# A two-layer decoder on one core: block ends without GpSimd's drain, transposed probabilities in the score banks, and a root computed two steps earlier

## What is computed

```python
x = x + linear_attention(layernorm(x))                    # layer 0
x = x + cross_attention_16_heads(layernorm(x), ctx)       # layer 0, head size 16
h = layernorm(x)                                          # layer 0, 16 experts
val, idx = top_k(sigmoid(h @ gate_w + gate_b), 2)
x = x + h + mlp_shared(h) + sum(val / sum(val) * expert[idx](h))
x = x + self_attention_16_heads(layernorm(x))             # layer 1, head size 64
# layer 1, cross attention with 8 heads of size 64, its own norms
q = (layernorm(layernorm(x)) * g1 + b1) @ Wq
k, v = split((layernorm(ctx) * g2 + b2) @ Wkv)
x = x + softmax(q k^T / 8) v @ Wout + bout
# layer 1, 8 experts with a capacity of int(1.2 * 2 * 112 / 8) = 33 rows each
x = x + experts_1(layernorm(x))
```

## Time and profile before

| | us |
|---|---|
| median of 3 runs | 1809.79 (1804.32 to 1810.95) |
| profiled execution | 1809.45 |
| its span | 1807.8 |

### The profile page before, as it was taken

One profiled execution on the slowest core, in us unless ns is written; L12 is line 12 of the kernel. 1 busy time (PEld: TensorE's weight loads), 2 busy tenths in 40 slices (PEclk: granted clock), 3 DMA queues, 4 the chain that ended last, 5 costly groups with the idle time before them and its releaser, 6 DMA issues. The chain is left out here.

```text
span 1807.8 us, 36461 instructions
## 1 busy us (share of the span) xinstructions
PE 1646.2 (91%) x12689; PEld 1358.2 (75%) x12689; DVE 1113.7 (62%) x2668; ACT 884.1 (49%) x2541; POOL 554.3 (31%) x846
## 2 busy tenths in 40 slices
PE   5997599999998888799999969999999889999998
PEld 3665467777776577588888757777777679999987
DVE  4776467777777544367777656666666544444464
ACT  2333356555555233155555544444444456666644
POOL 2122222443343334422221111233223256444410
PEclk8999689999999789999999979999999989999999
DMA  8000323444450353200000020000000031123001
GB/s 255 0 0 1 113 83 120 131 129 129 129 171 12 121 168 124 63 11 17 12 12 1 1 85 20 18 14 14 18 18 1 1 140 71 71 76 134 1 1 42
DMA packets 87549, 114.29 MB, mean 63 GB/s; under 512 B 4804, under 2 KB 76696, under 8 KB 87160
## 3 DMA queue, kind: packets, MB, share of 16 engines
q1 hardware_dynamic: 82280, 99.56, 17.0%
q0 software_dynamic: 5136, 12.98, 2.2%
HBM read 64.68 MB, written 47.84 MB: 62 GB/s over the span
## 5 line engine op out<-in xcount | busy, mean ns | idle before, releaser
L1051 ACT ACTIVATE wide<-ps,c_negmax 112x375 f32<-112x375 f32 x256 | 143.7, 581 | 2.1 <-DVE c_negmax L1157 2.1
L1262 PEld LDWEIGHTS ps<-const,wide 112*125 112x125 f32 x768 | 97.8, 193 | 47.2 <-DVE c_pT L1179 27.5
L1157 DVE TENSOR_REDUCE c_negmax<-ps 112x2 f32<-112x750 f32 x128 | 114.2, 934 | 25.4 <-PE ps L1293 25.4
L1262 PE MATMUL ps<-const,wide 112*125 112x112 f32 x768 | 116.1, 289 | 3.4 <-ACT wide L1051 2.0
L2101 PE MATMUL ps<-xnT,wide 128*128 128x224 f32 x512 | 108.6, 361 | 4.7 <-ACT e_gate_up L1877 4.3
L1893 ACT ACTIVATE s_probs<-ps,s_negmax 112x112 f32<-112x112 f32 x256 | 86.7, 364 | 37.2 <-DVE s_negmax L1959 37.2
L2101 PEld LDWEIGHTS ps<-xnT,wide 128*128 128x128 f32 x512 | 93.5, 190 | 9.8 <-ACT e_gate_up L1877 5.5
L1352 PE MATMUL ps<-parts 128*125 128x256 f32 (+1 forms) x480 | 91.0, 327 | 5.5 <-DVE X L1108 2.4
L3041 DVE TENSOR_TENSOR e_hid_low<-xnT,e_hid_high 128x528 fp32r<-128x528 f32 x56 | 41.2, 735 | 82.7 <-ACT e_hid_high L2941 82.7
L1039 ACT COPY c_pT<-ps 125x672 f32<-125x672 f32 x64 | 46.1, 720 | 82.0 <-PE ps L1262 82.0
L1352 PEld LDWEIGHTS ps<-parts 128*125 128x125 f32 (+1 forms) x480 | 71.8, 196 | 13.1 <-DVE wide L1103 4.7
(11 more groups left out here) (493 smaller groups left out, 5074.0 us busy)
## 6 DMA issues: line engine op xcount, KB each, us to landing
expert_rows<-d_zero SPq DMA_DIRECT2D x16, 2240.0 KB, 11.5
c_ctx_in<-in_ctx SPq DMA_DIRECT2D x32, 375.0 KB
e_x_in<-expert_rows SPq DMA_DIRECT2D x43, 128.0 KB, 2.1
expert_rows<-e_y POOLq DMA_DIRECT2D x43, 128.0 KB, 2.1
e_w_gate_even<-in_L_ffn_w_gate SPq DMA_DIRECT2D x4, 1024.0 KB, 5.1
e_w_fc_even<-in_L_ffn_w_c_fc SPq DMA_DIRECT2D x4, 1024.0 KB, 7.2
e_w_proj_even<-in_L_ffn_w_c_proj SPq DMA_DIRECT2D x4, 1024.0 KB, 9.6
c_kv<-in_L_ffn_w_gate SPq DMA_DIRECT2D x4, 1024.0 KB, 5.0
```

Of the source, the lines that this page charges most:

```text
L1051: last = nc.scalar.activation(probs[:, g % 2, r, :], ps[:T, r, 0:S], ACT.Exp, bias=negmax[:, par, h:h + 1], accum_out=sums[:, par, h:h + 1])
L1157: nc.vector.tensor_reduce(negmax[:, par, h:h + 3:2], ps[:T, 2 * piece:2 * piece + 2, 0:S], AX.X, ALU.max, negate=True).then_inc(max_done, 1)
L1262: last = nc.tensor.transpose(ps[:KC, bank + r % 2, k * T:(k + 1) * T], probs[:, g % 2, r, k * KC:(k + 1) * KC], ident[:T, :T])
```

## The change

In context attention 1 the transposed probabilities of head x go into score bank x instead of bank 4, and TensorE no longer waits for the copy before. In experts 0 the root moves from behind the store of block 33 to behind that of block 31, and `ContextEntry.STEPS` goes from 10 to 13, which moves the normalized rows from the steps 35 to 37 to the steps 38 to 40.

```diff
-        block = ctx.enter_context(nc.Block())
+        block = ctx.enter_context(nc.Block(no_gpsimd_drain=True))
...
-        with nc.Block() as block:
+        with nc.Block(no_gpsimd_drain=True) as block:
...
-                if j == CONTEXT_AT + 5:
+                if j == CONTEXT_AT + 3:
                     entry.power(pool, 0)
...
-    STEPS = 10
+    STEPS = 13
...
-    BANK_PT, BANK_O, BANK_SIDE = 4, 5, 6
+    BANK_O, BANK_SIDE = 5, 6
...
                     act.wait_ge(pT_mm, 4 * (2 * i + g) + x + 1)
-                    nc.scalar.copy(pT[:, x, :], ps[:KC, BANK_PT, 0:SC]).then_inc(pT_ready, 1)
+                    nc.scalar.copy(pT[:, x, :], ps[:KC, x, 0:SC]).then_inc(pT_ready, 1)
...
                     dve.wait_ge(pT_mm, 4 * (2 * i + g) + x + 1)
-                    nc.vector.tensor_copy(pT[:, x, :], ps[:KC, BANK_PT, 0:SC]).then_inc(pT_ready, 1)
+                    nc.vector.tensor_copy(pT[:, x, :], ps[:KC, x, 0:SC]).then_inc(pT_ready, 1)
...
                 pe.wait_ge(exp_done, n + 1)
-                if not (first(i, g) and x == 0):
-                    pe.wait_ge(pT_ready, n)
                 for k in range(NK):
-                    last = nc.tensor.transpose(ps[:KC, BANK_PT, k * T:(k + 1) * T], probs[:, x, k * KC:(k + 1) * KC], ident[:T, :T])
+                    last = nc.tensor.transpose(ps[:KC, x, k * T:(k + 1) * T], probs[:, x, k * KC:(k + 1) * KC], ident[:T, :T])
                 last.then_inc(pT_mm, 1)
```

## The result

| | before | after |
|---|---|---|
| median of 3 runs, us | 1809.79 | 1785.39 |
| lowest and highest | 1804.32 to 1810.95 | 1784.55 to 1786.39 |
| profiled execution, its span | 1809.45, 1807.8 | 1784.55, 1782.9 |

The account below looks back on a forecast made before the run. It took TensorE's pace to bound the two layer-one attention stages. 1809.45 - 10.9 (banks) - 1.85 (root) + 2.8 (block ends) = 1799.5 us, set to 1799.8 for the median; range 1788.5 to 1804.0.

Parts of the forecast that it names:

- Part 3, the block ends: At block ends without Pool's drain, L118's drain does the same work behind the first barrier: cost 2.8 us.
- nobody pays: At three block ends, the removed drain's time vanishes and L118's stays at 40 ns: -6.25 us, 1790.8 in all; chance 0.25.
- the 2 us of clock: In context attention 1's tail, fewer gaps may keep TensorE's higher clock: up to 2 us gained, taken as 0.
- Part 1, steady iterations: Context attention 1, iterations 1 to 13: no wait for the probabilities' copy, 0.44 us gained each, 5.7 us together.
- Its last iteration: Context attention 1, iteration 15: copies no longer waited for, values start 1.95 us earlier; 4.0 us gained over both halves.
- Part 2, the root: Experts 0: power runs earlier and rows later, so the 3.48 us step loses its wait; 1.85 us gained.
- The slower rival: After self-attention 1's longer pause, context attention stays at the lower clock; an iteration costs 17 us, 1816.8; chance 0.04.
- The beat stays: Context attention 1's steady iterations gain nothing, other waits replacing the stall; only the last two gain, 5.2 us: 1805.5; chance 0.11.

Follow-up runs that it names:

- the added meeting: The changed kernel with one more plain all-engine barrier in front of the clearing of the semaphores; 1800.59 us against 1785.39 of the changed kernel.

## Why the prediction was wrong

It forecast 1799.8 and a range of 1788.5 to 1804.0; measured 1785.4. By its own steps:

**Part 3, the block ends: the step that failed.** "So the likeliest result is that L118's drain does the same work": it took 0.04 to 0.06 us at every end instead of 2.4 to 4.2. The price of 84 ns for each of POOL's DMAs was right (83 to 90 measured), and so was that a plain drain behind the meeting pays it. The step passed over the resetting drain of L117, which stands ahead of L118's, and which the kernel's text shows. The trace of before couldn't tell what it costs or takes off, because there a plain drain had already done the work when it ran (0.054 to 0.116 us). It takes the work off, as the experiment with a resetting drain of an unused semaphore shows. So the ends gained 6.18 where 2.8 were to be lost: 9.0 of the 14.9 us that the forecast missed. The rival "nobody pays" has the ends' gain to 0.1 us, but its number is right by luck: its reasons, that the time was the removed instruction's own or that Pool does the work in the background, are refuted by the added meeting, where a plain drain pays in full. Its chance of 0.25 was too low all the same, since what could absorb the work stood in the code between the two drains. The ends alone don't explain the miss of the range either: that rival's time was 1790.8, and 1788.8 with the 2 us of clock that were left to the range.

**Part 1, steady iterations: right.** 0.44 forecast, 0.41 measured, with the wait of value2 for L2452 that the forecast named. **Its last iteration: mis-sized.** 4.0 forecast, 6.8 by the trace. The way to the value products shortened nearly as worked out (2.07 us in the first half, where 1.95 were forecast, and 2.41 in the second); the clock was taken at 0 with up to 2 us left to the range. It was worth 2.3 on the value and score products of the first half, and 2.8 if all that is beyond 4.0 is counted: TensorE stays at its higher level for most of the tail when the stalls are gone, and doesn't when they are put back. The stage's 13.05 is 5.4 in 13 iterations, 1.2 in the fourteenth, 6.8 in the last, less 0.4 lost at its start.

**Part 2, the root: right.** 1.85 forecast, 1.86 in the trace (step 37), and the rows at the steps 38 to 40 cost nothing: these steps are at 1.62 us as before.

**What was not in it: the other stages, mostly their clock.** Experts 0 was 7.02 shorter, of which 1.86 are the root's; 1.5 come at its start (the shorter pause), 1.9 in the steps 8 to 10 and 1.7 in 31 and 32, where the steps were at 3.20 and 3.03 us before and at 2.55 and 1.62 after. Linear attention gave 1.4 and self attention 1 took 2.74 back. Together 3.8 us less, of which only the 1.5 at the experts' start go with the change in most profiles; the rest is inside what two executions of one program differ by. That it came out as a gain is luck of the two profiles as far as the runs can tell. The medians are steadier: four more sessions have the kernel before at 1808.4 to 1809.9 us, though its single runs spread over 1801.3 to 1818.0.

**The slower rival** (the clock low over an iteration) didn't occur; the stage lost 0.4 us at its start. **"The beat stays"** is refuted by the period of 23.84 us.

The sum: 10.0 forecast + 9.0 (ends) + 2.1 (context attention 1) + 3.8 (the other stages, mostly clock) = 24.9 us, the distance of the two spans.

## What to carry to other kernels

When a drain is removed and another one stays, list every instruction that stands between them before you say who pays: here a semaphore-resetting drain in between made the work vanish, and one added drain in the kernel before would have shown it. GpSimd's first plain drain costs by the number of DMAs that GpSimd has issued since the last one, so leave it out of a block's end that all engines wait for, or put it where GpSimd has slack. And count a run of short stalls on TensorE at the clock that it has behind them, not only at their length.

## What the runs showed of the hardware that was not expected

- A plain drain of GpSimd costs 83 to 90 ns for each of GpSimd's DMAs since its last drain (28, 30 and 49 of them), also 100 us after the last of them; with none in between it takes 0.04 us.
- A semaphore-resetting drain in its place ends 0.06 us behind the last operation, takes 0.09 and 0.11 us at the changed kernel's ends of context attention 0 and self attention 1, ends 0.12 us behind the last gather at the experts', and leaves 0.04 to 0.06 us for a plain one behind it.
- The granted clock behind short stalls of TensorE: 0.62 over 19.6 us in the kernel that has six stalls of 0.2 to 0.8 us for the copies, 1.00 to 0.82 in the one without them; over the last 20 us 0.62 to 0.68 in seven profiles with them, 0.91 or 1.00 in seven without. Behind single pauses of about 2 us it differed between executions of the same program, 0.67, 0.89 and 0.68.
